# The last expert layer's first part moved into the stage woven before it, the first image worked off first

## The reference

```python
x = x + _L2_conv_ref(_ln_c(x), ...)     # depthwise 5x5 and dilated 3x3 with made kernels, then a fusing 1x1
t = t + _L2_ffn_ref(_ln_t(t), ...)      # product with signs of a weight, bias, clip, round to sevenths
x = x + _L3_conv_ref(_ln_c(x), ...)     # depthwise 3x3, relu, prune by the image's peak >= 4, 1x1, relu, prune
t = t + _L3_ffn_ref(_ln_t(t), ...)      # 8 experts, top 2: (silu(x w1) * (x w3)) w2, weighted and summed
```

## Time and profile before

| | us |
|---|---|
| median of the runs (1642.69 to 1645.54) | 1645.41 |
| the profiled execution | 1645.37 |
| its span | 1643.6 |
| TensorE busy | 1395.9 (85%) |
| VectorE busy | 936.7 (57%) |
| ScalarE busy | 799.2 (49%) |
| GpSimd busy | 528.6 (32%) |
| woven stage | 1230.4 to 1392.5 |
| last expert layer, first judge to first expert product | 1393.6 to 1446.6 |
| its expert tiles | 1446.6 to 1600 |
| its last fetches and the end | 1600 to 1643.6 |

### The profile page before, as it was taken

The page is one execution under the profiler, slowest core; times in us unless marked ns, Lnnn a source line. Parts: engine busy times, 40 slices in busy tenths (PEclk is TensorE's granted clock), DMA queues, the critical chain, the costliest instruction groups (busy, mean ns, idle before and its releaser), DMA issues. The chain is left out here.

```text
span 1643.6 us, 32527 instructions
## 1 busy us (share of the span) xinstructions
PE 1395.9 (85%) x10212; PEld 1305.3 (79%) x10212; DVE 936.7 (57%) x2527; ACT 799.2 (49%) x2316; POOL 528.6 (32%) x707
## 2 busy tenths in 40 slices
PE   3799998999997899975799998989956997369990
PEld 2799998999996899973599997879944974269980
DVE  6655466788655434543655556543337784655662
ACT  4211114444335877773444445466656643455540
POOL 2300007777415355532000000413340000547645
PEclk8899999999998899996899999989987999689995
DMA  6200000111212443410000000013313300224442
GB/s 227 67 1 1 1 8 21 27 27 27 90 49 65 160 136 106 114 53 22 0 1 1 1 1 1 30 48 100 81 42 63 63 1 17 94 84 145 134 131 73
DMA packets 102527, 95.01 MB, mean 58 GB/s; under 512 B 12616, under 2 KB 94164, under 8 KB 100960
## 3 DMA queue, kind: packets, MB, share of 16 engines
q1 hardware_dynamic: 90080, 64.27, 12.8%
q0 software_dynamic: 12288, 28.73, 6.5%
HBM read 46.42 MB, written 36.70 MB: 51 GB/s over the span
## 5 line engine op out<-in xcount | busy, mean ns | idle before, releaser
L1285 POOL DMA_INDIRECT slots<-U,m_slot_at x180 | 175.2, 973 | 360.2 <-DVE m_slot_at L1200 186.0
L1026 PE MATMUL m_pre<-m_xg,m_own 128*128 128x128 f32 x1888 | 256.0, 280 | 16.5 <-ACT m_h L1116 8.6
L1026 PEld LDWEIGHTS m_pre<-m_xg,m_own 128*128 128x128 f32 x1888 | 235.2, 196 | 20.1 <-issue 17.8
L1116 ACT ACTIVATE m_h<-m_pre,m_own 128x128 f32<-128x128 f32 x572 | 164.2, 374 | 60.9 <-PE m_pre L1026 60.8
L1643 PE MATMUL at_mixed<-at_v,at_probs 128*128 128x130 f32 x1296 | 178.3, 277 | 3.1 <-DVE at_normed L1741 2.3
L1643 PEld LDWEIGHTS at_mixed<-at_v,at_probs 128*128 128x128 f32 x1296 | 173.6, 192 | 7.7 <-ACT at_probs L1705 3.6
L1705 ACT ACTIVATE at_probs<-at_scores 128x384 f32<-128x384 f32 x216 | 105.4, 491 | 145.0 <-PE at_scores L1659 143.6
L1718 DVE TENSOR_REDUCE at_peaks<-at_sampled 128x1 f32<-128x512 f32 (+1 forms) x180 | 113.0, 635 | 57.3 <-PE at_sampled L1626 56.9
L1294 POOL DMA_INDIRECT U<-results,m_slot_at x108 | 104.1, 964 | 123.1 <-DMA results<-m_y 65.9
L1038 PE MATMUL m_out<-out_a,m_h 128*128 x744 | 100.1, 278 | 0.2 <-issue 0.2
L694 ACT ACTIVATE l_probs<-l_scores 126x384 f32<-126x384 f32 x96 | 47.1, 491 | 104.4 <-PE l_scores L573 104.4
(11 more groups left out here) (399 smaller groups left out, 3496.5 us busy)
## 6 DMA issues: line engine op xcount, KB each, us to landing
m_x_in<-slots SPq DMA_DIRECT2D x62, 256.0 KB, 3.2
results<-m_y SPq DMA_DIRECT2D x62, 256.0 KB, 2.5
slots<-zeros SPq DMA_DIRECT2D x3, 2048.0 KB, 15.7
l_queries<-l_parts SPq DMA_DIRECT2D x256, 18.0 KB, 1.9
slots<-U,m_slot_at POOLq DMA_INDIRECT x180, 2.2
dc_down_high<-dc_f_high POOLq DMA_DIRECT2D x8, 312.0 KB, 5.4
dc_down_low<-dc_f_low POOLq DMA_DIRECT2D x8, 312.0 KB, 9.2
X<-in_x SPq DMA_DIRECT2D x4, 576.0 KB, 5.5
```

The lines of the kernel that those rows point to most:

```text
L1026: last = pe.matmul(pre[n % 2][:, c * 128:(c + 1) * 128], own[n % RING][:, c * 128:(c + 1) * 128], xg[n % RING][:, :], start=True, stop=True)
L1116: last = act.activation(h[n % HELD][:, c * 128:(c + 1) * 128], pre[n % 2][:, c * 128:(c + 1) * 128], act_func, bias=own[n % RING][:, HID + ...
L1285: pool.indirect_dma_start(slots[b], bass.IndirectOffsetOnAxis(ap=slot_at[b][k][:, n:n + 1], axis=0), tokens[b][:, n, :], None).then_inc(la ...
```

## The change

1. **Parts by name.** `PARTS` gives way to `SHARES`, with a list of chunks for each expert layer; all loops take their part's own number of chunks, tiles and groups. The parts stay as they are: 12, 12, 12 for m1 and m7, 18, 18 for m3.
2. **m7 gets a lead of one part.** Judging, ranking and the first 22 sends of part 0 are written into the woven stage; parts 1 and 2 follow at `END + 1` and `END + 27`, the experts at `END + 5`. The judge works on a single PSUM bank (`pre`) there. A semaphore `tile_final` tells that a tile of `X` is final.
3. **First image first.** `PLAN` has new times: image 0 is mixed, chosen and added before image 1's depthwise work. The final addition of image 0 is cut into four tiles and a rest. Mixing of image 0 uses one bank, that of image 1 `product` and `norms[0].back`.
4. The last layer's weights are loaded by SP within the woven stage, after six convolution tiles and after the third gather block. The two split copies of the features share one tensor with the features (`F`, `f`).
5. **Weights of the picks** are a program of their own (`weigh`), for m7 not before `END + 14`.
6. m1's second rank moves from `OC * 11 - 0.2` to `OC * 12 - 0.2` (OC = 6.2, one output convolution tile), that is behind the last convolution. The due times of fetched rows are spread by 7 us a tile where the next part has begun.

```diff
-PARTS = {1: 2, 2: 3}
+SHARES = {"m1": (12, 12, 12), "m3": (18, 18), "m7": (12, 12, 12)}
+TOP = {"m1": 2, "m3": 1, "m7": 2}
...
-        following, loads = follow(Lead(judge_at, 2, (OC * 7 - 0.2, OC * 11 - 0.2), 2, END, 0, OC * 7 + 1.0, 1.3), x_ready, send_paced)
+        following, loads = follow(Lead(judge_at, 2, (OC * 7 - 0.2, OC * 12 - 0.2), 2, END, 0, OC * 7 + 1.0, 1.3), x_ready, send_paced)
...
-    weights_at = [judged_at[b] + (8.5 if lead else 16.0) for b in range(parts)]
+    weights_at = [max(judged_at[b] + 8.5, lead.weigh_after) if lead else judged_at[b] + 16.0 for b in range(parts)]
...
-        return max(expert_at[b + 1] + 6.0, expert_at[0] + begun((parts - 1 + b) * MOVES + i * MOVES // TP) * COST) + 2.0
+        move = len(paced_sends) + (chunk_of[b] + i * CH) * top
+        return max(expert_at[b + 1] + 6.0 + 7.0 * max(i - 1, 0), expert_at[0] + begun(move) * COST) + 2.0
...
     def scalar_program(act):
+        def weigh(b):
+            yield weights_at[b]
+            act.wait_ge(exp_in[b], 1)
+            if not renormalise:
+                act.activation(below_peak[b][:, :, :], below_peak[b][:, :, :], ACT.Exp).then_inc(exp_out[b], 1)
+            act.activation(behind[b][:, :], behind[b][:, :], ACT.Exp).then_inc(exp_out[b], 1)
...
-        return Programs(*[part(b) for b in both])
+        return Programs(*[part(b) for b in both], *[weigh(b) for b in both if top == 2])
...
-    "mixed": (133.86, 137.66, 138.51, 139.36, 140.21, 141.06, 141.91, 142.76, 143.61, 144.46, 145.31, 146.16),
+    "mixed": (115.59, 117.28, 119.45, 121.06, 122.67, 124.28, 166.9, 167.75, 168.6, 169.45, 170.3, 171.15),
...
-    "gather": ((72.97, 74.31, 75.9, 80.24, 81.83, 82.88, 85.29, 87.82, 89.16), (90.95, 93.53, 96.68, 98.47, 100.06, 104.46, 106.87, 107.92, 110.82), (112.41, 113.58, 115.17, 119.57, 120.91, 124.06, 125.11, 126.16, 127.33)),
+    "gather": ((71.69, 72.86, 74.45, 76.04, 77.38, 78.72, 79.89, 81.06, 82.65), (85.67, 87.08, 88.67, 89.84, 91.01, 92.6, 94.19, 95.78, 97.37), (98.54, 100.13, 101.54, 102.95, 104.12, 105.71, 107.3, 108.64, 109.81)),
...
-    "weigh": (131.3, 139.09),
-    "choose": (143.19, 149.38),
-    "final": (144.13, 149.96),
-    "spread_first": (90.82, 115.89, 128.88),
-    "depthwise": (106.82, 113.98, 119.96, 124.95, 130.76, 134.56),
-    "spread": (110.07, 117.23, 123.21, 128.2, 134.01, 137.81),
+    "weigh": (114.38, 166.02),
+    "choose": (126.75, 173.28),
+    "final": ((127.87, 128.59, 129.47, 130.69, 132.99), (173.86,)),
+    "spread_first": (83.7, 98.42, 110.86),
+    "depthwise": (134.68, 140.91, 147.8, 153.73, 158.24, 161.49),
+    "spread": (137.93, 144.93, 151.05, 156.98, 161.49, 164.74),
...
+    "judge": (128.59, 130.19, 132.32, 133.93),
+    "rank": 144.01,
+    "send": 148.64,
+    "end": 177.01,
...
+        following.banks([pre, pre], [])
+        EARLY = sum(SHARES["m7"][:1]) // CH
...
-            return (pre, product)[t % 2]
+            return pre if t < TB else (product, norms[0].back)[t % 2]
...
-                        yield at["final"][b]
-                        rows = slice(b * H, (b + 1) * H)
-                        dve.scalar_tensor_tensor(X[:, rows, :], H1[:, rows, :], keep[:, 1, b:b + 1], X[:, rows, :], ALU.mult, ALU.add)
+                        cuts = [i * TR for i in range(EARLY + 1)] + [H] if b == 0 else [H, ROWS]
+                        for i, (first, end) in enumerate(zip(cuts, cuts[1:])):
+                            yield at["final"][b][i]
+                            rows = slice(first, end)
+                            dve.scalar_tensor_tensor(X[:, rows, :], H1[:, rows, :], keep[:, 1, b:b + 1], X[:, rows, :], ALU.mult, ALU.add).then_inc(tile_final, 1)
...
+                following.engines.gpsimd.run(END)
                 pool.wait_ge(moved, 16 * 8 * B)
...
-                tensor_program(pe).run()
+                following.engines.tensor.alongside(tensor_program(pe).steps(), END)
...
+            @block.sync
+            def _(sp):
+                sp.wait_ge(conv_ready, TB)
+                sp.dma_start(loads[0][0], loads[0][1]).then_inc(loads[0][2], 16)
+                sp.wait_ge(acc_ready, 3)
+                sp.dma_start(loads[1][0], loads[1][1]).then_inc(loads[1][2], 16)
+                following.engines.sync.run(END)
...
+        lead = Lead(lambda b, t: PLAN["judge"][t], 1, (PLAN["rank"],), 1, END, 0, PLAN["send"], 1.3, weigh_after=END + 14.0)
```

## The result

The changed kernel takes 1653.01 us (1650.61 to 1655.86), the kernel before 1645.41 on the same chip: a ratio of 1.0044, with an interval of 1.0034 to 1.0054. That is 7.6 us slower, where 6.9 us faster was forecast. The profiled execution has a span of 1652.2 us, 8.6 more than before.

The account below looks back on a forecast made before the run. The last expert layer's lead-in was taken to wait on judging, ranking and 24 GpSimd sends, its tiles on TensorE. 1645.4 - 19.3 (lead-in) + 11.5 (part 2) + 1.2 (part 1) - 0.3 (layer 0) = 1638.5 us; range 1628 to 1651.

Parts of the forecast that it names:

- the depthwise run: Woven stage: image 1's depthwise tiles would take 44.6 us from first start to last end, near the 45.0 of now.
- C: Rival, woven stage: TensorE's clock falls in image 0's finish, three depthwise tiles take 11.6 us each; +17, 1656 us; chance 0.12.
- D: Rival, woven stage: GpSimd's sends crawl beside a busy VectorE, each three times as long; 1687 us; chance 0.02.
- E: Rival, woven stage: part 0's sends wait and run after the barrier, 28 us more; 1666 us; chance 0.03.
- I take the lead of 5 us over: Woven stage: up to the last gather step (planned 110.9) work stays 5 us ahead of plan; first depthwise product about 128.6.
- 1.4 us more: Lead-in: two judge tiles of part 1 rather than one, between token load and first expert product, cost this at low clock.
- The sum by gaps: Expert tiles: part 2 judged wholly inside costs 11.5 us (bounds 5 and 15), part 1 another 1.2.
- 0.3 us: Layer 0's end: with the rank moved, the stage ends only this much earlier, as GpSimd's sends and VectorE run on.
- nothing: Layer 1: later fetch dates move additions by two tiles inside a stretch that TensorE binds, so no time changes.
- With the rank behind the last convolution this goes: Layer 0's end: TensorE's 3.58 us idle before the rank, and the half clock behind it, would vanish.
- A: Rival, expert tiles: the inner part costs little (5 us) and the woven stage meets its early bound; 1628 us; chance 0.17.
- B: Rival: gain cancels, plan met rather than beaten (first depthwise product at 135) plus a late barrier; 1646 us; chance 0.21.

Follow-up runs that it names:

- a_again: The changed kernel, unchanged, run again as reference on a chip without the stalls: ratio 1.0035 to the kernel before.
- a_more_picks: The changed kernel with twelve more pick-like VectorE instructions (3.5 us) in one unbroken run with part 2's picks: ratio 1.0206 to the kernel before.
- a_tables_3: The changed kernel without ScalarE's four table loads for part 2 of the last layer (normalisation and weights left out): ratio 1.0033 to the kernel before.
- b_rank12: The kernel before with only m1's second rank moved behind the last convolution (OC * 12): 1648.87 us against 1645.23.
- sets 1, 3 and 4: Follow-up runs, variants of the changed kernel and one of the kernel before itself, on chips with stalls; the kernel before takes 1728 us there.
- sets 2, 5 and 6: Follow-up runs, variants of both kernels, on chips without the stalls; the kernel before takes 1645 us there.

## Why the prediction was wrong, step by step

**What bounds the kernel, and the depthwise run: right.** The lead-in did fall by 40 us, the sends were hidden (two behind the barrier, as forecast), depthwise took 44.8 us for 44.6 and the last tail 11.3 for 11.8. C is wrong at its place: depthwise ran at the full clock. D and E are wrong: 0.96 us a send, 22 inside. D's row was misread, though: the send at 1482.52 lies beside a product of gate and value, and its neighbours, which do lie beside copies, take longer (1.05 us at 1481.07 and 1483.97). Kernel before, GpSimd and VectorE:

```profile
1483.97 1.05 POOL L1285 DMA_INDIRECT slots<-U,m_slot_at  x1 [0.49 <-PE m_pre L1026]
```

```profile
1484.48 0.42 DVE L1241 COPY m_own<-in 128x512 f32 x1
```

So where the Trainium skill has a VectorE copy lock GpSimd out (SBUF — State Buffer, "SBUF: two separate sides"), these rows show 0.1 us a send (1.05 against 0.96), nowhere near the threefold price of D.

**The first depthwise product: 3.2 us late.** The step that failed is "I take the lead of 5 us over". The last gather step ends at 108.5 on the plan's scale, 2.5 ahead of its plan and not 5. The price of a step, 1.04 us, was read where three stand side by side; in the changed queue other steps of VectorE stand between them:

```profile
1339.14 1.01 DVE L2333 SCALAR_TENSOR_TENSOR dc_acc<-XP,params_sb,dc_acc 128x768 f32<-128x768 f32 x1
...
1343.17 0.99 DVE L2333 SCALAR_TENSOR_TENSOR dc_acc<-XP,params_sb,dc_acc 128x768 f32<-128x768 f32 x1
```

Over these last three distances the trace takes 4.03 us and the plan 4.10, so no lead grows there. Nor was the lead of 5 there at the last gather step before the change: that step started 0.4 us behind its plan. Why the lead grew to 2.3 us only stays open. The chain behind it took 23.3 us for 21 to 22: six mixing tiles 1.67 apart and judge tiles 1.6 to 2.2 apart for 1.4.

**The lead-in: 3.1 us late.** Its price for the judge tiles, "1.4 us more", was that of six products. A judge tile on a single bank costs products and copy, 2.3 at the low clock, and two of them stood behind the tokens: from the last send's start to the first product it took 10.7 us where 8.5 were planned. The other 0.9 is the barrier: the first of the two sends came 2.05 us behind the stage's end, for 1.1. The diff showed that one bank is passed for the lead; I did not follow `turned_banks` into the parts outside it.

**The tiles: 4.5 us too cheap in this trace, 3.5 in a_again's.** The sum by gaps gave 12.7, its bounds 6 to 16; 17.2 came, all in part 0's 31 tiles. VectorE's work in them grew by 12.3 us (36.66 to 48.91), ScalarE's by 10.9. TensorE's waits grew by 10.5 and its own work by 6.7, where the sum had about 4 for judge tiles, rank and the tile more of part 1. In a_again the waits are the same (17.4 us in all) and its work is 56.15 and not 58.95: so 2.8 us of the error are a lower granted clock in the first tiles, which the forecast had no term for and which isn't there in every profile. The rest are waits that the sum left out, the judge tiles' two waits for their bank (1.2 us) among them. By a_more_picks work on VectorE costs its length, by a_tables_3 the table loads half of theirs.

**Layers 0 and 1: "0.3 us", "nothing", and no bound.** The step "With the rank behind the last convolution this goes" failed twice. The idle time was not the rank's: it stays, 4.41 us, in front of the last convolution. And the step left out what the rank releases: b_rank12 shows slots, codes and weights pushed to the barrier and beyond. The clock at m3's end added another 2 to 3, by chance as far as the runs tell.

**The rivals.** A is wrong: the tiles cost 17.2 us more and not 5. B's sign came true (a first depthwise product after 1366), but neither its time (1646) nor its reason: the plan was beaten by 2.9 us. Each of the four terms was off by 3 to 5 us to the same side, and the range had let only two of them move. Most of it has one root: each step was costed by its own instructions, and the waits that go with them (a bank, a copy, a successor on another engine) were counted only where the old trace happened to show them. The clock's part, at m3's end and in the first tiles, doesn't come from there.

## What to carry to other kernels

A step moved in a queue takes everything that it releases along; write down what waits for it on each other engine before pricing the idle time that it leaves. Work that helper engines do among tiles bound by one engine isn't free: here it was paid at half to all of its length, and cutting it up changed nothing by itself. So a lead-in of 40 us won at the front can come back as 27 us of stage and 17 us of tiles; here it paid only once sends, banks and the order of the later parts were set anew together, and the clock helped. And a train of indirect sends that is free in an idle stretch may not be free beside work on every chip.

## What the runs showed of the hardware

- On the chips of sets 1, 3 and 4 ScalarE stands still during trains of indirect DMAs from GpSimd (30.9 us beside a train of 30.2; 17.8 beside one of 27.7). It waits for TensorE's semaphore, whose event stands 21 and 12 us behind the recorded end of the products, against 0.02 on the other chips; why is open. The same programs show none of it on the chips of sets 2, 5 and 6. The kernel before takes 1728 us there and 1645 here.
- The same chain of norm steps runs at either level of TensorE's clock from one build to another, 3.32 or 4.29 us a round, with the same instructions around it.
- A table load on ScalarE takes 1.28 us and the next activation starts 0.01 us behind it. Four loads fewer made 31 tiles 2.6 us shorter.
- A GpSimd indirect send takes 0.96 us, and 1.05 in the two rows named above beside a VectorE copy within SBUF.
- Two profiles of one kernel differ by 2.9 us in the first four expert tiles alone (17.4 and 14.5 us to the first store), with the mean granted clock of the 31 tiles at 0.94 and 0.98.
